# Layer 1's low-rank factor and router computed token by token, with five smaller edits of order, buffers and loads

## Time and profile before

| | us |
|---|---|
| runs | 1156.78, 1156.51, 1156.80 |
| median | 1156.78 |
| profiled execution | 1158.54 |
| its span, first to last instruction | 1156.7 |
| TensorE busy in the span | 1101.9 |

### The profile page before, as it was taken

One profiled execution on the slowest core, in us unless ns is written; L12 is line 12 of the kernel. 1 busy time (PEld: TensorE's weight loads), 2 busy tenths in 40 slices (PEclk: granted clock), 3 DMA queues, 4 the chain that ended last, 5 costly groups with the idle time before them and its releaser, 6 DMA issues.

```text
span 1156.7 us, 47306 instructions
## 1 busy us (share of the span) xinstructions
PE 1101.9 (95%) x22032; PEld 796.1 (69%) x22032; DVE 539.2 (47%) x1157; ACT 332.1 (29%) x705; POOL 509.2 (44%) x380
## 2 busy tenths in 40 slices
PE   5899999999999999999999999999998999999997
PEld 4456777777766777777667777677676776776765
DVE  5774555344544444544444354544333354443343
ACT  2323333133332223223223223323221223222221
POOL 2536736345634544355353551465444243654300
PEclk9999999999999999999999999999999999999999
DMA  5455300010514000002124000003223000001011
GB/s 148 172 193 175 114 3 2 3 47 22 202 58 147 3 3 3 2 3 103 75 75 148 4 3 2 3 2 103 76 75 109 5 3 3 2 3 75 3 38 37
DMA packets 22307, 64.92 MB, mean 56 GB/s; under 512 B 4768, under 2 KB 5856, under 8 KB 17888
## 3 DMA queue, kind: packets, MB, share of 16 engines
q1 hardware_dynamic: 20576, 61.50, 14.8%
q10 hardware_dynamic: 1536, 0.40, 0.2%
HBM read 44.07 MB, written 17.83 MB: 54 GB/s over the span
## 4 chain that ended last, share of the span: by engine, by line
PE 76%; DVE 13%; issue 2%; DMA 2%; ACT 0%; DVEq 0%
PE bank_a L1554 14%; PE bank_b L1554 14%; PE bank_a L108 10%; PE bank_b L108 9%; PE bank_a L91 5%; DVE y L1248 4%; PE bank_b L91 2%; PE bank_b L67 2%; PE bank_a L67 2%; PE bank_b L79 2%; PE bank_a L79 2%; DVE y3t_lo L1303 2%; DMA out_x<-out_tile 2%; PE bank_b L1512 1%; PE bank_a L1512 1%
## 5 line engine op out<-in xcount | busy, mean ns | idle before, releaser
L1120 POOL TENSOR_TENSOR xs<-x,tab 128x512 f32<-128x512 f32 x96 | 112.4, 1179 | 418.1 <-DVE x L1317 418.1
L1107 POOL TENSOR_TENSOR sums<-raw 128x896 f32<-128x896 f32 x62 | 128.5, 2094 | 73.8 <-ACT raw L1158 73.8
L108 PE MATMUL bank_a<-y,wv 32*64 32x256 f32 x4096 | 119.9, 380 | 3.5 <-issue 3.5
L108 PE MATMUL bank_b<-y,wv 32*64 32x256 f32 x4096 | 115.5, 375 | 2.8 <-issue 2.8
L1554 PE MATMUL bank_b<-w_hi,y3t_hi 128*128 128x512 f32 x256 | 106.2, 415 | 6.7 <-DVE y3t_lo L1303 5.1
L1554 PE MATMUL bank_a<-w_hi,y3t_hi 128*128 128x512 f32 x256 | 106.5, 416 | 4.0 <-DVE y3t_lo L1303 3.4
L108 PEld LDWEIGHTS bank_a<-y,wv 32*64 32x64 f32 x4096 | 94.5, 132 | 21.9 <-issue 6.8
L108 PEld LDWEIGHTS bank_b<-y,wv 32*64 32x64 f32 x4096 | 94.0, 130 | 18.2 <-issue 4.1
L1554 PE MATMUL bank_a<-w_lo,y3t_hi 128*128 128x512 f32 x256 | 101.1, 395 | 0.0
L1554 PE MATMUL bank_b<-w_lo,y3t_hi 128*128 128x512 f32 x256 | 100.8, 394 | 0.0
L1136 POOL TENSOR_TENSOR x<-x,ob 128x512 f32<-128x512 f32 x64 | 80.0, 1285 | 0.0
(11 more groups left out here) (320 smaller groups left out, 1963.3 us busy)
## 6 DMA issues: line engine op xcount, KB each, us to landing
w_hi<-w_scratch SPq DMA_DIRECT2D x9, 1024.0 KB, 5.8
w_lo<-w_scratch SPq DMA_DIRECT2D x9, 1024.0 KB, 8.2
x_in<-in_x SPq DMA_DIRECT2D x32, 256.0 KB, 4.3
out_x<-out_tile SPq DMA_DIRECT2D x32, 256.0 KB, 2.3
w_raw<-in_w SPq DMA_DIRECT2D x3, 1024.0 KB, 8.7
w_scratch<-w_hi SPq DMA_DIRECT2D x3, 1024.0 KB, 4.1
w_scratch<-w_lo SPq DMA_DIRECT2D x3, 1024.0 KB, 7.9
w_raw<-w_scratch SPq DMA_DIRECT2D x2, 1024.0 KB, 9.5
```

What stands on the lines that cost most here:

```text
L108: last = pe.matmul(banks[b][2 * CH * h:2 * CH * (h + 1), HALF * u:HALF * (u + 1)], keep["wv"][rows, a, SPAN - q:SPAN - q + 2].rearrange("p ...
L1107: g_.tensor_tensor(sums[i][:], pairs[:, :, one[0], one[1]:one[1] + SPAN], pairs[:, :, other[0], other[1]:other[1] + SPAN], ALU.add).then_i ...
L1120: nc.gpsimd.tensor_tensor(xs[:, b, 1:LEN + 1], src[:, b], column(n, T_S, b).broadcast_to((P, LEN)), ALU.mult).then_inc(xs_ready, 1)
```

## The change

- Layer 1's adapter: hi and lo of the factor and the router stand side by side in one tile `ar1` of 2 x 136 columns, `[a1 hi 128 | r1 hi 8 | a1 lo 128 | r1 lo 8]`. For each quarter t of 128 tokens, the turned tokens are stationary: four matmuls of `y3t_hi` against all 272 columns and four of `y3t_lo` against the first 136, into one bank each: three in `conv_banks(m + 1)`, one in `lin_banks(m)`. ScalarE copies the lo columns to `z_both`, VectorE adds the hi columns (`both_parts`). The sums have the tokens on the partitions at once; `to_tokens` does nothing in layer 1. `inner_product`, which writes the same banks, waits for `both_parts`.
- Ends: `te` takes the table unscaled (one VectorE instruction instead of two), and is added to the convolution's sums in PSUM, four small additions ahead of `y3`. ScalarE and VectorE write `y3` after that; `turn` waits for `y3` alone.
- Results of layer 3 are written in `x` itself; the stores read `x`, and GpSimd waits for the stores before it writes the next group's `x`.
- `load_weights` issues eight DMAs of 256 KB, each when the one before it has landed. The load for layer 0 goes behind the stores of the phase.
- Layers 0 and 2: `edge1` moves behind base 1 and `effective`, `edge2` behind base 2. `edge1` then uses a bank of `lin_banks`.
- VectorE's head: first bank of `evacuate_0`, quarter 0 of `turned`, second bank, quarter 1.

```diff
-Z1 = E1 * R1 + 2 * E1
+A1 = E1 * R1 + E1
...
+    def z_tokens_ps(m, t):
+        return z_ps(m) if t == ROWS - 1 else conv_banks(m + 1)[1 + t]
+
+    def edge_1_ps(n):
+        return conv_banks(n)[0] if layer(n - 1) in (1, 3) else lin_banks(n - 1)[0]
...
             def load_weights(u, l):
+                landed = 16 * 2 * KB * (loads(u) - 1)
                 for i in range(2):
-                    sp.dma_start(w[u % 2][i][:].bitcast(F32), scratch["w"][i, l]).then_inc(w_loaded[u % 2], 16)
+                    for k in range(KB):
+                        if landed:
+                            sp.wait_ge(w_loaded[u % 2], landed)
+                        sp.dma_start(w[u % 2][i][:, k].bitcast(F32), scratch["w"][i, l, :, k]).then_inc(w_loaded[u % 2], 16)
+                        landed += 16
...
+                            if n >= STEP:
+                                pool.wait_ge(stored[g], 16 * ROWS * (n // STEP))
                         nc.gpsimd.tensor_tensor(x[g][:, b], src[:, b], keep["ob"][:, l], ALU.add).then_inc(xb_ready, 1)
...
                 if l == 1:
-                    a.activation(z_raw[:], z_ps(m)[:], ACT.Copy)
-                    a.activation(logits[0:2 * E1], logit_ps(m)[0:2 * E1], ACT.Copy).then_inc(z_raw_ready, 1)
+                    for t in range(ROWS):
+                        act.wait_ge(zq_done, ROWS * before(m, (1,)) + t + 1)
+                        a.activation(z_both[:, t], z_tokens_ps(m, t)[:, A1:2 * A1], ACT.Copy).then_inc(zq_raw, 1)
...
             def evacuate_3(n):
                 dve.wait_ge(cc_done, n + 1)
+                for b in (*ON_ACT, *ON_DVE):
+                    ends = conv_banks(n)[b][:].rearrange("p (u i) -> p u i", u=2)[:, :, 0:HALF:HALF - 1]
+                    v.tensor_tensor(ends, ends, te[:, b], ALU.add).then_inc(ends_ready, 1)
+                dve.wait_ge(ends_ready, tiles(n, ROWS))
...
-                dve.wait_ge(y3_act, tiles(n, ROWS))
-                dve.wait_ge(y3_dve, tiles(n, ROWS))
-                ends = y3[:, :, :, 0:HALF:HALF - 1]
-                v.tensor_tensor(ends, ends, te[:].rearrange("p e u b -> p b u e"), ALU.add).then_inc(ends_ready, 1)
...
+            def both_parts(m):
+                if layer(m) != 1:
+                    return
+                for t in range(ROWS):
+                    dve.wait_ge(zq_raw, ROWS * before(m, (1,)) + t + 1)
+                    v.tensor_tensor(z_both[:, t], z_tokens_ps(m, t)[:, 0:A1], z_both[:, t], ALU.add).then_inc(zq_ready, 1)
...
             def inner_product(n):
-                pe.wait_ge(b_e_ready, n)
+                if layer(n - 2) in (1, 3):
+                    pe.wait_ge(b_e_ready, n)
+                if layer(n - 2) == 1:
+                    pe.wait_ge(zq_ready, tiles(before(n - 2, (1,)) + 1, 0))
...
             def adapter(m):
                 l = layer(m)
+                if l == 1:
+                    for t in range(ROWS):
+                        pe.wait_ge(y3t_lo, tiles(m, 2 if t < 2 else KB))
+                        for part, width in ((0, 2 * A1), (1, A1)):
+                            for k in range(KB):
+                                ins = pe.matmul(z_tokens_ps(m, t)[:, 0:width], y3t[part][:, k, P * t:P * (t + 1)],
+                                                keep["ar1"][:, k, 0:width],
+                                                start=(part == 0 and k == 0), stop=(part == 1 and k == KB - 1))
+                        ins.then_inc(zq_done, 1)
+                    return
...
                 else:
                     base(m, 1)
-                    edge2(n)
                     effective(m, 0)
+                    edge1(n)
                     inner_product(n + 1)
...
                     base(m, 2)
+                    edge2(n)
                     outer_product(n + 1)
```

More of the change, by code:

```diff
@@ L650, in bias_3 @@
                     scale = table[:, :, l, T_O:T_O + 2]
[L651 to L654, removed]
+                    for kind in (1, 2):
+                        v.tensor_copy(table[:, :, l, T_E + 2 * kind - 2:T_E + 2 * kind],
+                                      bias3_ps[l][:, kind].rearrange("p u (i c) -> p i u c", i=ITERS))
+                    then(v.tensor_tensor(table[:, :, l, T_BO:T_BO + 2], scale,
+                                         bias3_ps[l][:, 0].rearrange("p u (i c) -> p i u c", i=ITERS), ALU.mult))
                     out = table[:, :, l, T_BO:T_BO + 2]
@@ L1086, in _ @@
                         sp.wait_ge(x_ready, tiles(m, b + 1))
[L1087 removed]
+                        sp.dma_start(io["out"][group(m)][:, b], x[m % 2][:, b]).then_inc(stored[m % 2], 16)
+                if n % STEP == STEP - 1 and it + 1 < ITERS:
+                    sp.wait_ge(lin_done, tiles(n - 1, 0))
+                    sp.wait_ge(w_kept, 32 * 3)
+                    load_weights(USES * (it + 1), 0)
             for u in range(2):
[L1089 removed]
+                sp.wait_ge(stored[u], 16 * ROWS * ITERS)
         @block.gpsimd
@@ L1161, in evacuate_3 @@
             def evacuate_3(n):
-                act.wait_ge(cc_done, n + 1)
-                for b in ON_ACT:
+                for i, b in enumerate(ON_ACT):
+                    act.wait_ge(ends_ready, tiles(n, i + 1))
                     for u in range(2):
@@ L1421, in _ @@
                         last_taps(n)
+                    both_parts(m)
+                    if convolve:
                         edges_2(n)
@@ L1459, in edge1 @@
                 pe.wait_ge(y0_e_ready, n + 1)
-                edge_1(pe, conv_banks(n)[0], keep, layer(n)).then_inc(e1_done, 1)
+                if layer(n - 1) in (0, 2):
+                    pe.wait_ge(x_ready, tiles(n - 1, 1))
+                edge_1(pe, edge_1_ps(n), keep, layer(n)).then_inc(e1_done, 1)
             def edge2(n):
@@ L1496, in adapter @@
                 l = layer(m)
-                pe.wait_ge(y3t_hi, tiles(m, KB))
-                if l == 1:
-                    for part, factors in ((0, (0, 1)), (1, (0,))):
-                        if part:
-                            pe.wait_ge(y3t_lo, tiles(m, KB))
-                        for k in range(KB):
-                            for ai in factors:
-                                pe.matmul(z_ps(m)[:], keep["a1"][ai][:, k], y3t[part][:, k],
-                                          start=(part == 0 and k == 0 and ai == 0), stop=(part == 1 and k == KB - 1))
-                ps, columns_, weights_ = (logit_ps(m), 2 * E1, keep["r1"]) if l == 1 else (z_ps(m), 2 * Z23, keep["a3"])
+                if l == 1:
[8 more added lines that the diff above has]
+                    return
+                pe.wait_ge(y3t_hi, tiles(m, KB))
                 for part in range(2):
@@ L1532, in to_tokens @@
                 l = layer(m)
-                pe.wait_ge(z_raw_ready, before(m, (1, 3)) + 1)
+                if l == 1:
+                    return
+                pe.wait_ge(z_raw_ready, before(m, (3,)) + 1)
                 for t in range(ROWS):
```

128 lines of the change are left out of this document (53 added, 75 removed).

## The result

The changed kernel takes 1114.5 us (median; 1110.5 to 1117.6) where the kernel before takes 1156.8: a ratio of 0.962, 95% interval 0.960 to 0.964. The prediction was 1125 with 1115 as its low end, so the gain of 42.3 us fell just outside its range. The profiled execution took 1112.61 us with a span of 1110.8 and a granted clock of 0.994, 45.9 us under the one of before.

The account below looks back on a forecast made before the run. TensorE, busy 95% of the span, was taken as the bound. Terms 8.7 + 5.3 + 4.5 + 3.0 + 3.0 + 7.5 = 32.0 us off 1158.54 gave 1126.5; the runs' median, 1.76 lower, made it 1125; range 1115 to 1146.

Parts of the forecast that it names:

- the rivals: Chances: narrow matmuls stay costly (1140 us) 0.2; stalls stay (1132) 0.15; loads late, slower 0.04; ends stay on path (1135) 0.06.
- Adapter: Layer 1, 8 phases: narrow matmuls without transposes shorten the stage, less a stall before the inner product; 1.09 us each, 8.7 together.
- Ends in PSUM: Between conv0 and turn in 13 phases: small additions ahead of y3 end the wait for the ends; gain 5.3 us.
- VectorE's head: Start of base 0 after turn: one bank ahead of the first quarter saves 0.25 us in 18 phases, 4.5 us.
- Results in x: Before edge3 in 7 phases: the third residual no longer waits for a store; gain 3.0 us.
- Order, layers 0 and 2: In 16 phases: small blocks join others, so one pair of tile-shape changes goes; 0.19 us each, 3.0 us together.
- Paced loads: Conv0 or span beside weight loads, five places: 256 KB at a time removes 7.5 of 12.4 us of TensorE stalls.
- conv0 at 3.34 us in every phase: Sign that the forecast is right: conv0, up to the start of turn, as short in every phase as in phase 10.
- Copy and add: Layer 1, before the inner product: ScalarE's copy about 0.31 us and VectorE's addition about 0.25, within a 0.65 us stall.
- a piece of a load: SP's queue: each of eight 256 KB pieces of a weight load takes about 3 us, 24 us for a load.

## Why the prediction was wrong

The direction and most of the mechanisms were right, none of the rivals came, and the sum was too small: 32.0 us against 45.9 in the profiled executions. Gains in us; the middle column from stages, the last from ratios (good to 3 or so); edits undone one at a time need not add up, but the middle column nearly does (47).

| Term | Predicted | Stages | Ratios |
|---|---|---|---|
| Adapter | 8.7 | 11.7 | 17.4, with the next |
| Place of the weight tiles | none | 3.8 | 3.1 |
| Ends in PSUM | 5.3 | 6.9, less 2.6 | 0.6 |
| VectorE's head | 4.5 | 6.5, less 1.9 | 4.1 |
| Results in x | 3.0 | 4.1 | 4.9 |
| Order, layers 0 and 2 | 3.0 | 5.8 | 5.1 |
| Paced loads | 7.5 | 12.9 | 12.5 |

- **Paced loads** is the step that failed most. It said that three spans stall without a load, "so 7.5 us of the 12.4". Undone, the pacing costs 12.5 us, the whole of that excess. The three spans show that something else stalls TensorE too; they do not show that pieces of 256 KB do. A discount was taken from a row that did not bear on it. That 12.5 us came back where 12.4 had been read is partly luck: the stalls beside loads fall in other stages, with other lengths, from kernel to kernel.
- **The order** took 0.19 us for one change of shape in each of 16 phases. That is right for eight (0.21); in the phases with `effective` it is 0.45, since that block joins the wide ones as well.
- **The adapter** came to 1.46 us a phase instead of 1.09. The stage was 3.94 us instead of 4.22, because 136 and 272 columns pace at 0.10 and 0.1375 us where the sum had 0.11 and 0.143; the stall was 0.58 for 0.65, the wait behind the outer product gave 0.31 for 0.26, and the old transposes had taken 0.85 for 0.88.
- **The place of the weight tiles** had no step. The change takes tiles out of SBUF ahead of them, and their new start happens to match the turned activations' modulo 256 bytes.
- **Ends and head** have the right mechanism: `turn` waits for `y3` in no phase but the last, and base 0 follows 2.1 us after it from phase 2 on. The sign "conv0 at 3.34 us in every phase" did not come: phases 5, 6, 26 and 28 are still 0.2 to 0.8 us longer. Both gains were larger in their own stage and had a price that the prediction did not name, the wait of edge 1 in layer 1 for `y_e`. That wait is 2.6 us in the first profile of the kernel after, 1.7 in the second, 0.7 with the head undone and none with the ends undone: both edits together make it, so its price stands in both rows of the table.
- **Smaller readings.** Copy and add took 0.28 and 0.30 us for the predicted 0.31 and 0.25, and a piece of a load 3.2 for 3.

The terms that were too small all erred to the same side, and the range's low end allowed 10 us for all of them together. 3.8 of the 13.9 us missed had no term at all.

## What to carry to other kernels

A large load whose time is not pressing goes in pieces, each behind the one before, sized so that the pieces still come in time: here 2 MB at once cost 12.5 us against pieces of 256 KB, and pieces of 128 KB came too late and cost 51. When tiles are taken out of SBUF, look where the ones behind them land, and compare a stage that nobody touched. A wait that was added as a whole often needs only a part: waiting for three of four adds gave 4.7 us for one line.

## What was not expected of the hardware

- fp32r matmuls of 512 columns were about 1% faster (mean of one 390 instead of 395 ns; the fourth twelve of a phase 2.75 to 2.76 instead of 2.78 to 2.80 us in layer 1, 2.76 to 2.77 instead of 2.79 to 2.81 in layer 3), where the moving and the stationary tile start at the same offset modulo 256 bytes of a partition. Offsets of 0, 64, 96, 128 and 192 against 224 were slow; 224 with 224, 0 with 0 and 480 with 224 fast.
- Narrow fp32r matmuls with a fresh 128-column tile each pace at 0.10 us (136 columns) and 0.1375 us (272), with their loads beside them.
- Beside 1 MB loads the instruction queue's next packet started 5.9 us into a span instead of 3.0, and TensorE stood for 1.91 and 2.14 us.
- A stall of TensorE in a span can be paid twice: after 2.14 us of standing, with the granted clock down to 0.55 in the mean, the next 38 records took 2.54 us instead of 1.05. After 1.91 us of standing the clock stayed at 1.00, and 38 took 1.45 us all the same.
